# Gated recurrence with a mixture of experts on one Trainium2 core: the experts of tiles 0 to 11 computed by routed blocks in place of all eight densely, cn kept whole in fp32, and the tile loop written out

## The reference, cut to what matters

```python
retained = (qt * r).reshape(B, D)
inp = retained @ Wi.T + bi
gate = sigmoid(inp @ Wg.T + bg)
state = tanh((gate * state + (1 - gate) * inp) @ A.T + inp @ Bm.T)   # 128 steps
out = state @ Wo.T + bo
x = x + tanh(g_xattn) * out
fx = layernorm(x)
shared_out = swiglu(fx @ w_shared_in) @ w_shared_out
top_val, top_idx = top_k(softmax(fx @ w_gate + gate_bias), 2)
wdense = zeros(S, 8) with top_val added at top_idx
hid = swiglu(fx @ w1_shared)
routed_out = sum over e of wdense[:, e] * (hid @ w2[e])
x = x + tanh(g_ffn) * (shared_out + routed_out)
```

## Time and profile before

| | us |
|---|---|
| median of 3 runs | 514.4 |
| the profiled execution | 515.2 |
| its span, on which all rows lie | 513.4 |
| TensorE matmul busy | 482.4 (94%) |
| VectorE busy | 422.7 (82%) |
| ScalarE busy | 221.2 (43%) |
| GpSimd busy | 122.7 (24%) |

### The profile page before, as it was taken

How to read it: one execution, slowest core, us unless ns; L and a number is a source line. 1 busy time by engine, 2 the same in 40 slices (tenths; PEclk the granted TensorE clock), 3 DMA queues, 4 the chain that set the end, 5 groups by cost and what they waited for, 6 DMA issues and landing times.

```text
span 513.4 us, 12634 instructions
## 1 busy us (share of the span) xinstructions
PE 482.4 (94%) x4574; PEld 365.5 (71%) x4574; DVE 422.7 (82%) x1438; ACT 221.2 (43%) x516; POOL 122.7 (24%) x149
## 2 busy tenths in 40 slices
PE   5977668999999999999999999999999999989996
PEld 4865556687777777787877777777778787756562
DVE  3788774989798888889898989888888979696966
ACT  3665567344353444453543535444535343233120
POOL 3001472231222212221312222122222131121210
PEclk8998788999999999999999999999999999999999
DMA  7772002020302002020202020110210101000001
GB/s 162 192 214 60 1 1 62 1 63 23 63 2 63 20 25 57 20 61 20 61 20 61 8 63 11 45 37 20 61 41 2 42 2 30 14 2 22 20 1 41
DMA packets 46064, 22.05 MB, mean 43 GB/s; under 512 B 35665, under 2 KB 39377, under 8 KB 46033
## 3 DMA queue, kind: packets, MB, share of 16 engines
q1 hardware_dynamic: 45904, 21.65, 16.7%
q0 software_dynamic: 128, 0.00, 0.1%
HBM read 17.45 MB, written 4.19 MB: 42 GB/s over the span
## 4 chain that ended last, share of the span: by engine, by line
PE 80%; DVE 10%; ACT 2%; issue 2%; POOL 0%; DVEq 0%; ACTq 0%
PE bank L466 35%; PE bank L455 24%; PE rec L455 8%; PE rec L480 5%; PE rec L485 3%; PE bank L524 1%; PE bank L512 1%; DVE u_hi L1088 1%; DVE u_full L1090 1%; DVE acc L1106 1%; DVE acc L1109 1%; PE bank L624 1%; DVE w2max L1060 1%; PE bank L747 1%; DVE x L1178 1%
## 5 line engine op out<-in xcount | busy, mean ns | idle before, releaser
L777 ACT ACTIVATE state<-rec 128x64 f32<-128x64 f32 x128 | 36.6, 286 | 178.1 <-PE rec L485 177.5
L466 PE MATMUL bank<-w_hi,hid_hi 128*128 128x512 f16 x256 | 97.4, 380 | 2.5 <-DVE acc L1109 1.7
L466 PE MATMUL bank<-w_lo,hid_hi 128*128 128x512 f16 x256 | 97.1, 379 | 0.0
L466 PE MATMUL bank<-w_hi,hid_lo 128*128 128x512 f16 x256 | 97.1, 379 | 0.0
L1088 DVE SCALAR_TENSOR_TENSOR u_hi<-gt,state 128x64 f16<-128x64 f32 x127 | 36.9, 291 | 53.7 <-ACT state L777 53.0
L1109 DVE SCALAR_TENSOR_TENSOR acc<-bank,wts,acc 128x256 f32<-128x256 f32 x128 | 62.0, 484 | 4.6
L1106 DVE SCALAR_TENSOR_TENSOR acc<-bank,wts,acc 128x256 f32<-128x256 f32 x128 | 60.7, 474 | 1.6 <-PE bank L466 1.5
L480 PE MATMUL rec<-u_hi,a_hi 128*128 128x32 f16 x512 | 47.6, 194 | 10.5 <-DVE u_hi L1088 10.5
L480 PEld LDWEIGHTS rec<-u_hi,a_hi 128*128 128x128 f16 x512 | 38.1, 98 | 20.4 <-DVE u_hi L1088 12.9
L480 PE MATMUL rec<-u_hi,a_lo 128*128 128x32 f16 x512 | 47.5, 194 | 0.0
L466 PEld LDWEIGHTS bank<-w_hi,hid_lo 128*128 128x128 f16 x256 | 25.0, 98 | 30.2
(11 more groups left out here) (223 smaller groups left out, 1391.7 us busy)
## 6 DMA issues: line engine op xcount, KB each, us to landing
x_sb<-in_x_dram SPq DMA_DIRECT2D x16, 256.0 KB, 3.3
c_sb<-in_ctx_dram SPq DMA_DIRECT2D x64, 64.0 KB, 3.0
xr_sb<-in_x_dram SPq DMA_DIRECT2D x16, 256.0 KB, 3.4
out_dram<-acc SPq DMA_DIRECT2D x16, 256.0 KB, 2.5
raw_w<-in_L_ffn_w_dram SPq DMA_DIRECT2D x8, 256.0 KB, 4.6
raw_sh<-n_L_ffn_w_shared_in_dram SPq DMA_DIRECT2D x1, 512.0 KB, 6.3
raw_w<-in_L_ffn_w_shared_dram SPq DMA_DIRECT2D x1, 512.0 KB, 6.7
raw_Wi<-in_L_xattn_Wi_dram SPq DMA_DIRECT2D x1, 256.0 KB, 3.3
```

What stands on the lines that cost most here:

```text
L466: last = pe.matmul(dst, a[:, kc, s * P:(s + 1) * P], w(part, kc), start=first, stop=(kc == KC - 1 and a is a_lo), skip_group_check=True)
L777: act.activation(step_of(state[i % 2], t), step_of(rec[i % 2], t), ACT.Tanh, scale=1.0 / PSCALE).then_inc(st_ready[t], 1)
```

## The change

Tiles 0 to 11 form three chunks of four tiles. For them the dense pairs are gone. In place of them:

- ScalarE and GpSimd write hi and lo halves of `hid` in token rows (`hid_rows`); `w1` is computed with tokens on partitions, its first half in slot 7 and its second in slot 0 of the next iteration.
- After the last tile of a chunk, `prefix` (TensorE), `places` and `rows` (VectorE, iterations 5, 9 and 13) compute each (token, pick) pair's row in a table sorted by expert and padded to blocks of 128 rows, and the expert number of each block, eight numbers packed in an integer.
- GpSimd scatters: 16 indirect DMAs for a chunk, each 128 rows of 1 KB, to `hrows` in DRAM.
- The SP queue reads two blocks at a time back, transposed. TensorE runs a `duo` for each (12 a chunk, 36 in all): it reads the expert number into a register and does 6 matmuls of 256 columns for a block, 23 blocks a chunk. ScalarE copies the result out, the SP queue stores it to `yrows`, and GpSimd gathers 16 times a chunk. VectorE adds a tile in four operations.
- Duos stand in iterations 8, 9, 10, 12 and 13 (slots 0, 2, 4, 5), in 14 and 15 (slots 0, 2), and twelve, the whole last chunk, in 16 (two in each of slots 0 to 5).
- At the start ScalarE's queue zeroes both `hrows`: 2 x 23 x 128 rows of 1 KB.
- `cn` is multiplied whole in fp32, in 4 matmuls; `cn_hi` and `cn_lo` are gone. The loop is written out. `addend_bm` moves to slot 5. `top_at`, `hot` move ahead, `hid` back.

```diff
+CHUNKS = ((0, 4), (4, 4), (8, 4))
+DENSE = 12
+IDS = 8
+def blocks_of(q):
+    return 4 * CHUNKS[q][1] + E - 1
...
         def run(eng, iteration):
-            for i in range(1, FIRST_FULL):
-                iteration(i, Static())
-            with eng.Fori(FIRST_FULL // 2, LAST_FULL // 2) as reg:
...
+            for i in range(1, LAST):
+                iteration(i, first)
+        for n, at in enumerate([(i, slot) for i in (8, 9, 10, 12, 13) for slot in (0, 2, 4, 5)]
+                               + [(i, slot) for i in (14, 15) for slot in (0, 2)]
+                               + [(16, slot) for slot in range(6) for _ in range(2)]):
+        COMBINE = {12: (0,), 13: (1,), 14: (2,), 15: (3,), 16: (4, 5), 17: (6, 7), 18: (8, 9, 10, 11)}
...
+            def turn_rows(n):
+                q, j, blocks = duo_chunk(n)
+                if j == 0:
+                    sp.wait_ge(scattered, 16 * 4 * (last_of(q) + 1))
...
+                    sp.wait_ge(duo_done, n - RING + 1)
+                sp.dma_start_transpose(hid_t[n % RING][:, :, 0:blocks * P],
+                                       hrows[q % 2][2 * P * j:2 * P * j + blocks * P, :]).then_inc(ht_in[n % RING], 16)
+            def duo(n, dst):
+                pe.wait_ge(ht_in[n % RING], 16 * (n // RING + 1))
...
+                    if at % IDS == 0:
+                        word[0] = pe.value_load(table[q][0:1, at // IDS:at // IDS + 1], min_val=0, max_val=E ** IDS - 1)
+                    e = pe.snap((word[0] >> (3 * (at % IDS))) & (E - 1))
+                    for kc in range(KC):
+                        for part, half in ((0, 0), (1, 0), (0, 1)):
+                            last = pe.matmul(dst[:, b * D:(b + 1) * D], hid_t[n % RING][:, half * KC + kc, b * P:(b + 1) * P],
+                                             split["w2"][part][:, kc, bass.ds(e, 1), :].rearrange("p a b -> p (a b)"),
...
-                feature_product(flat(rec[a % 2][:, :, :]), "a", cn_s[a % 2], False).then_inc(ac_done, 1)
+                for oc in range(KC):
+                    for kc in range(KC):
+                        last = pe.matmul(rec[a % 2][:, oc, :], whole_a[:, kc, oc * P:(oc + 1) * P], cn[a % 2][:, kc, :],
...
+            act.wait_ge(zeros_ready, 1)
+            for n in range(2):
+                act.dma_start(hrows[n].rearrange("(b p) d -> p b d", p=P),
+                              zeros[:, :].unsqueeze(1).to_broadcast([P, MOST_BLOCKS, 2 * D])).then_inc(zeroed, 16)
...
+                    act.copy(y_sb[n % RING][:, cols], duo_bank(n, i, slot)[:, cols]).then_inc(y_ready, 1)
...
+            def scatter(t, s, pick):
+                pool.indirect_dma_start(hrows[q % 2], bass.IndirectOffsetOnAxis(ap=slots_i[q][:, at:at + 1], axis=0),
+                                        hid_rows[t % 6][:, s, :, :].rearrange("p a d -> p (a d)"), None,
+            def gather(t, s, pick):
+                if t == CHUNKS[q][0] and s == 0 and pick == 0:
+                    for r in range(RING):
+                        pool.wait_ge(y_out[r], 16 * IN_RING[q][r])
+                if t >= 4 and s == 0 and pick == 0:
+                    pool.wait_ge(combined, t - 3)
+                pool.indirect_dma_start(yg[t % 4][:, s, pick, :], None, yrows[q % 2],
...
+                spread(SCATTERS, range(t, t + n), [(i, 5)] * 4 + [(i + 1, 3)] + [(i + 1, 4)] * 3 + [(i + 1, 5)] * 4
+                       + [(i + 2, 3)] + [(i + 2, 4)] * 3)
+            spread(GATHERS, range(0, 4), [(11, 5)] * 4 + [(12, 3)] + [(12, 4)] * 3 + [(12, 5)] * 4 + [(13, 3)] + [(13, 4)] * 3)
+            spread(GATHERS, range(4, 8), [(15, 5)] * 4 + [(16, 4)] * 12)
+            spread(GATHERS, range(8, 12), [(17, 5)] * 16)
```

More of the change, by code:

```diff
@@ L300, in tile @@
                 return m
[L302 to L333, removed]
@@ L352, in gated_layer, with duo_bank, duo_chunk, evacuated @@
+        def duo_bank(n, i, slot):
+            if i < TILES:
+                return bank[{0: 2, 2: 3, 4: 4, 5: 5}[slot]][:, :]
+            return flat(rec[n % 2][:, :, :])
+        def duo_chunk(n):
+            q = next(q for q in range(len(CHUNKS)) if n < duos_before(q + 1))
+            j = n - duos_before(q)
+            return q, j, min(2, blocks_of(q) - 2 * j)
+        def evacuated(i, slot):
+            return max(n for at, ns in DUOS.items() if at <= (i, slot) for n in ns) + 1
         first = Static()
@@ L677, in iteration @@
                     last.then_inc(so_done, 1)
-                if k.has(e):
+                duos_at(i, 2)
+                for q in range(len(CHUNKS)):
+                    if d == last_of(q):
+                        if k.has(a):
+                            pe.wait_ge(ret_ready, k.n(a))
+                        prefix(q)
+                if k.dense(e):
                     if k.has(a):
@@ L1452, in iteration @@
                 add_pair(1, d, k)
+                for q in range(len(CHUNKS)):
+                    if d == last_of(q):
+                        rows(q)
                 gated_state(i, 6, k)
@@ new lines, in _, with spread @@
+            SCATTERS, GATHERS = {}, {}
+            def spread(plan, tiles, spots):
+                rows = [(t, s, pick) for t in tiles for s in range(HALVES) for pick in range(2)]
+                for row, at in zip(rows, spots, strict=True):
+                    plan.setdefault(at, []).append(row)
+            for q, (t, n) in enumerate(CHUNKS):
+                i = last_of(q) + 2
+                spread(SCATTERS, range(t, t + n), [(i, 5)] * 4 + [(i + 1, 3)] + [(i + 1, 4)] * 3 + [(i + 1, 5)] * 4
+                       + [(i + 2, 3)] + [(i + 2, 4)] * 3)
@@ L1541, in iteration @@
             def iteration(i, k):
                 a, c, d, f = i + 1, i - 1, i - 2, i + 2
[L1543 removed]
+                ahead = i == 1
                 if k.has(c):
@@ L1571, in iteration @@
                         w2_low(expert)
-                if k.static and i == 2:
+                if i == 2:
                     for expert in range(6, E):
                         w2_low(expert)
-                if not ahead:
-                    cn_low(a, k)
                 x_rstd(f, k)
+                moves(i, 5)
                 if ahead:
```

653 lines of the change are left out of this document (461 added, 192 removed).

## The result

The kernel after takes 520.5 us (median of 5 runs, 518.5 to 524.4) beside 514.5 us for the kernel before on the same chip: ratio 1.012, interval [1.007, 1.018]. The forecast was 475 us, with 452 to 512 as its range: wrong in sign and size. The profiled execution took 524.4 us, the longest of the five; its span is 522.7.

What follows compares the result with a forecast made beforehand. TensorE was taken as the bound before. To the last tanh, 107 + 100 + 23 + 122 + 27 + 25.4 = 404.5 us; with a 68 us tail, 472.5; plus 1.0 and 1.5, 475 us. Range 452 to 512.

Steps and rivals of the forecast that it cites:

- TensorE's sum: TensorE's work over the whole kernel: pairs removed, duos and smaller work added, -60 us in all.
- cn: Product with cn on TensorE in whole fp32: +0.45 us a tile, +7 us in all.
- Register work: Register reads and choice of expert on TensorE: 0.3 us a duo, +11 us, ends 0 and +36.
- The non-duo iteration: Iterations 3, 4, 6, 7 and 11, without pairs or duos: 20.0 us each, 100 us together.
- the longest way through the slots: Non-duo iteration: TensorE and VectorE waiting on each other slot by slot add about 0.9 us to TensorE's 18.1.
- the norm chain: Second layer norm's chain from recurrence 2: 6.7 us against 5.7 of TensorE's own slots, +1.0 us an iteration.
- The bound of 18.1 to 24: Ends for a non-duo iteration's length: 18.1 us with all hidden, 24 with VectorE held up by GpSimd.
- The start: Zeroing of 6 MB before iteration 3's first tanh: counted as 0 us, ends 0 and +15.
- The tail: After the last tanh: last gathers wait for combined until 51 us, then gathers, landing, adds and store; 68 us, +25.
- rival C: DMA late: zeroing delays w2, or transposed reads delay duos, above all in iteration 16; +15, 490 us, chance 0.09.
- B: Iterations 5 to 15: GpSimd's scatters and gathers hold up VectorE, 0.86 us each; +25 to +30, 502 us, chance 0.20.
- D: GpSimd becomes the bound at 2.4 us an indirect DMA, slower from about 2.1; 529 us, chance 0.13.

Runs made afterwards that it cites:

- 7: Kernel after, with nine useless matmuls on TensorE before the inp product of iterations 3 to 7 and 11: 522.1 us, ratio 1.015.
- 1: Kernel after, with VectorE making ret_lo ahead of the projection in slot 2, iterations 2 and later: 510.4 us, ratio 0.987.
- 10: Kernel of 9, with VectorE's blend in slot 5 put behind xn_lo: 486.6 us, ratio 0.941.
- kernel of 4: Kernel after, with ret_lo first, the zeroing on SP's queue and seven buffers for gathered rows: 495.6 us, ratio 0.961.
- 3: Kernel after, with seven buffers for gathered rows in place of four: 508.0 us in one run, 517.1 to 518.5 in three others, no ratio given.
- run 2: Kernel after, with the two zeroing DMAs issued by SP's queue in place of ScalarE's: 512.7 us, ratio 0.997.
- run 11: Kernel of 10, with ScalarE in place of SP starting the stores of duo results in iteration 16: 487.8 us, ratio 0.947.
- 9: Kernel of 4, with the adds of tiles 4 to 7 moved into iteration 16, 8 and 9 into 17, 10 and 11 in 18: 489.2 us, ratio 0.949.
- run 8: Kernel of 4, with the 48 scatters left out, so duos compute on zeroed rows: 492.7 us, ratio 0.956.

## Why the prediction was wrong, point by point

**TensorE's sum was right.** A duo's twelve matmuls take 1.3 us, the five duo iterations 124.3 us for a forecast of 122, iteration 15 25.9 for 25.4, iteration 14 29.0 for 27. cn was over-priced (0.28 us a tile for 0.45). Register work I can't see apart; with 0.3 us a duo for it the five iterations come out within 2.3 us.

**The non-duo iteration is the step that failed, the largest of three**: "the longest way through the slots is about 0.9 above 18.1", and "+1.0" for the norm chain; 20.0 was forecast, 24.6 came in iteration 4. The runs take the difference apart: 1.4 us for the clock (7: 24.59 to 23.20, as in iteration 3), 1.0 for the `ret_lo` wait itself (1: to 22.17), 0.8 for `blend` ahead of `xn_lo` (10: to 21.40). The last 1.4 us weren't separated; in iteration 4 of the kernel of 4 TensorE still waits 0.85 us for ScalarE's `xn` and 0.44 for `ret_lo`. The prediction gave one mean to VectorE's excess and left out what each product waits for: it never asked of each product what its operand waits for once the pair in front of it is gone. The pair had hidden two orders, `projected` before `ret_low` and `blend` before `xn_lo`, which cost nothing in a kernel bound by TensorE. With them in their better order the iteration that was forecast at 20.0 takes 21.4. The bound of 18.1 to 24 did not reach the 24.6 to 25.2 of iterations 4, 6 and 7. It had no term for the clock: without the 1.4 us these iterations would have been 23.2 to 23.8. Here idle TensorE had a price beyond the idle time.

**The start**: "I count 0; the ends are 0 and +15". I argued from bandwidth, and the hold is on the issuing queue: 9.35 us on ScalarE. The end held it, the value didn't (7.7 us in this profile, 3.6 to 5.3 in those of runs 1, 3 and 7; in run 2 it was gone when the DMAs were moved). I should have asked of each added DMA what stands behind it on its engine.

**The tail**: the mechanism was right (gathers behind `combined`, adds, store), the place was off by 11 us (61.9 for 51) and its price nearly right: an indirect DMA takes 1.04 us (gather) or 1.09 (scatter) and 0.30 to the next, 1.3 for 1.2; landing took 3.75 us. Part of what I missed is that duos of iteration 16 wait for transposed reads; in the chain of the kernel after 7.46 us are such a read, of which SP's queue was held for 1.45:

```profile
455.55 2.36 PE rec L612 x22
457.91 7.46 DMA raw_sh<-hrows
...
457.91 1.45 SPq L472 DMA_TRANSPOSE raw_sh<-hrows  x1
```

TensorE stood idle for 2.97 us of it. This was rival C's place, in iteration 16, and by run 11 it is the landing more than the issue. The prediction's 5 us for such a read was the median's size (4.5) but not that of the reads in iteration 16. That VectorE's adds stood in the wrong gaps is shown in part by 9. Its tail of 69.0 us is the forecast's 68, but that agreement is luck: it took edits that the forecast didn't have. The other parts of the 11 us weren't separated.

**The rivals.** B (GpSimd disturbs VectorE) has its sign and, for the scatters, about a fifth of its size: 5 us of length in run 8. B named the indirect DMAs, and a pass of another kind did more: behind the start of `hid_rows`, `ret_lo` took up to 1.63 us in place of 0.69 in nearly every iteration, which is 0.9 us of each stop of 2.0 us. The Trainium skill (GPSIMD Engine Reference, Key points) has VectorE's operations with two SBUF inputs contend with GpSimd; the trace agrees for GpSimd's elementwise passes, and run 8 shows the scatters' share to be small. D (GpSimd the bound) needed 2.1 us or more for an indirect DMA; with 1.3 it falls. Slower came out, but not by D: I had given 0.13 to the right sign for a wrong reason. C holds in part. For the landing of a gather the estimate from the Trainium skill (DMA: Bandwidth & Descriptors, Anatomy of one DMA) was 2.3 us; the gathers landed in about 3.8, and the measurement decides.

With all five orders mended (kernel of 10) the span is 483.6 us against the forecast's 472.5: 9.5 more in iterations 3 to 13, 3.3 more in 14 and 15, and the rest within 1 us. So the change together with the new order of the work around it is worth some 28 us on this kernel, and alone it costs 6. What the same edits of order would give on the kernel before was not measured; its waits for `ret_lo`, 1.2 us in all, say that this one would give little there.

## What to carry to other kernels

When a change empties the engine that bounds, go through every product that is left and ask which operand it waits for now and what stands ahead of that operand's maker in its own engine; a large filler hides bad orders that cost nothing while it is there. Here two swaps on VectorE were worth 10 and 3 us. Ask of every DMA added which engine's queue starts it and what is next in that stream: bytes are cheap where the queue is not. Rows that arrive early are worth nothing until the engine that uses them has a gap placed for them.

## What the runs showed of the hardware

- A DMA of 3 MB onto DRAM rows can hold the queue that starts it: in the kernel after the first took 0.49 us of ScalarE's, the second 9.35 (7.2 to 8.9 in three other profiles); on SP the pair took 6.68. A transposed read of 256 KB held SP for 1.2 to 3.7 us, 1.3 in the median; its landing took about 4.5 us in the median, and 7.46 and 13.92 for the two shown above.
- In iterations 4, 6 and 7 a stop of 2.0 us on TensorE was followed by some 3 us at half the granted clock (0.21 us a matmul in place of 0.12), that is 1.4 us more. Iterations 3 and 11 with the same stop kept 1.00, so not every such stop does this. In iteration 5 the stop was 1.0 us and the clock stayed up behind it; it fell later, behind the wait of 1.2 us for `xn_lo`.
- A VectorE operation (`ret_lo`) that started 0.07 us behind GpSimd's elementwise pass over a 128x512 tile took 1.63 us in place of 0.69. When it started 0.05 us ahead of the pass, it took 0.68 and the pass 1.65 in place of 1.15: the later of the two was the one stretched. Each scatter cost the iterations 0.1 us.
